# Last attention unit of a fused attention and long-convolution kernel: VectorE's queue reordered, four softmax products and one weight rest moved to GpSimd

## The reference

```python
h = einsum('bct,bcd->bdt', x, weights[condition])       # mixes the 32 channels
q_c = h @ Wq_c.T + bq_c;  q = (q_c @ Wq_up.T + bq_up)    # 32 heads of 128 + 64
kv = h @ Wkv_c.T + bkv_c                                 # latent 64 + rope 64
k_nope, v = split(kv[..., :64] @ Wkv_up.T + bkv_up)
attn = softmax(q . concat(k_nope, k_rope) / sqrt(192))   # 32 x 32 per row and head
x = x + (attn @ v) @ Wo.T, summed over the heads, + bo
y = mask * (causal_convolution(mask * x, kernel_of_channel) + D * mask * x)
x = x + y @ dequantized(qweight).T + bias
```

## Time and profile before

| | us |
|---|---|
| median of 3 timed runs | 732.34 (731.35 to 732.41) |
| the profiled execution, its own time | 729.96 |
| its span, first to last instruction | 728.1 |
| PE busy | 705.8 (97%) |
| VectorE busy | 601.3 (83%) |
| ACT busy | 412.7 (57%) |
| GpSimd busy | 208.1 (29%) |

### The profile page before, as it was taken

How to read it: one execution, slowest core, us unless ns; L and a number is a source line. 1 busy time by engine, 2 the same in 40 slices (tenths; PEclk the granted TensorE clock), 3 DMA queues, 4 the chain that set the end, 5 groups by cost and what they waited for, 6 DMA issues and landing times.

```text
span 728.1 us, 17041 instructions
## 1 busy us (share of the span) xinstructions
PE 705.8 (97%) x7154; PEld 567.8 (78%) x7154; DVE 601.3 (83%) x1010; ACT 412.7 (57%) x736; POOL 208.1 (29%) x237
## 2 busy tenths in 40 slices
PE   8999999999999999999999999999988899999997
PEld 6867777786978697777878786978666688888885
DVE  4889999998999777797769776787889689999975
ACT  4676565656556765746475565656645444444443
POOL 5461020020002010640110000004300257777784
PEclk9999999999999999999999999999999999999999
DMA  7800100010002001000100010002112487989943
GB/s 225 322 3 2 58 7 1 2 62 3 1 2 62 3 2 49 11 5 13 59 5 1 2 59 2 2 1 92 59 60 54 121 234 147 187 236 196 238 104 109
DMA packets 31919, 50.94 MB, mean 70 GB/s; under 512 B 6594, under 2 KB 21090, under 8 KB 30562
## 3 DMA queue, kind: packets, MB, share of 16 engines
q1 hardware_dynamic: 29858, 49.26, 25.0%
q0 software_dynamic: 1024, 0.53, 0.3%
q10 hardware_dynamic: 960, 0.06, 0.1%
HBM read 41.19 MB, written 8.63 MB: 68 GB/s over the span
## 4 chain that ended last, share of the span: by engine, by line
PE 72%; DVE 15%; issue 4%; ACT 4%; DMA 3%; POOL 2%; SPq 0%; DVEq 0%; ACTq 0%; POOLq 0%
PE ps L729 32%; PE ps L778 6%; PE ps L621 5%; PE ps L622 5%; PE ps L623 5%; PE ps L800 4%; PE ps L670 3%; PE ps L629 2%; PE ps L631 2%; PE ps L630 2%; DVE x_low L1654 2%; DVE x_t L1648 2%; PE ps L1022 1%; PE ps L1030 1%; DMA x_t<-in_x_channels 1%
## 5 line engine op out<-in xcount | busy, mean ns | idle before, releaser
L1134 ACT ACTIVATE qt<-ps,m_bias 128x512 f32<-128x512 f32 x228 | 145.9, 687 | 87.7 <-PE ps L729 86.9
L729 PE MATMUL ps<-q_high,m_high 64*128 64x512 f32 x768 | 165.0, 397 | 0.0
L729 PE MATMUL ps<-q_high,m_low 64*128 64x512 f32 x768 | 161.3, 387 | 0.0
L729 PE MATMUL ps<-q_low,m_high 64*128 64x512 f32 x768 | 113.8, 387 | 0.0
L729 PEld LDWEIGHTS ps<-q_high,m_high 64*128 64x128 f32 x768 | 88.7, 184 | 15.0 <-issue 5.5
L729 PEld LDWEIGHTS ps<-q_high,m_low 64*128 64x128 f32 x768 | 88.8, 184 | 9.2
L1422 DVE TENSOR_TENSOR z_low<-ps,z_high 128x512 fp32r<-128x512 f32 x128 | 79.8, 683 | 18.1 <-ACT z_high L1154 16.5
L729 PEld LDWEIGHTS ps<-q_low,m_high 64*128 64x128 f32 x768 | 81.1, 184 | 10.2
L1154 ACT CAST z_high<-ps 128x512 fp32r<-128x512 f32 x128 | 66.8, 597 | 14.6 <-PE ps L800 9.8
L1139 ACT ACTIVATE sc<-sc 128x512 f32<-128x512 f32 x60 | 38.1, 635 | 41.5 <-DVE sc L1407 41.4
L494 POOL TENSOR_TENSOR o_sum<-o_part,o_part 128x512 f32<-128x512 f32 x7 | 9.1, 1300 | 173.2 <-ACT o_part L1164 173.2
(11 more groups left out here) (259 smaller groups left out, 1468.7 us busy)
## 6 DMA issues: line engine op xcount, KB each, us to landing
x_raw<-in_x_groups SPq DMA_DIRECT2D x32, 256.0 KB, 4.0
x_t<-in_x_channels SPq DMA_DIRECT2D x8, 1024.0 KB, 7.9
out<-rest SPq DMA_DIRECT2D x32, 256.0 KB, 6.3
toep_high<-taps_scratch SPq DMA_DIRECT2D x32, 192.0 KB, 4.5
toep_low<-taps_scratch SPq DMA_DIRECT2D x32, 192.0 KB, 4.9
w_raw<-in_w_groups SPq DMA_DIRECT2D x8, 512.0 KB, 7.5
toep_far<-taps_scratch SPq DMA_DIRECT2D x32, 64.0 KB, 5.7
rope_raw<-in_rope_rows SPq DMA_DIRECT2D x8, 192.0 KB, 7.4
```

The costliest lines, as they stand in the source:

```text
L729: mm = pe.matmul(ps[:, fold_bank(u, j) + e, :], weights[rows, (GH * g + j) // 2, c, :], moving[c][rows, :], start=start, stop=stop)
L1134: act.activation(qt[:, j, :], ps[:, fold_bank(u, j) + j % 2, :], ACT.Identity, bias=m_bias[:, h:h + 1]).then_inc(s["qt_done"], 1)
```

## The change

On VectorE, ended_last is split into summed_last (sum and reciprocal) and turned_last (only the transpose, which now waits for the product by norm_done). Quarter 1 is begun directly behind quarter 0, and the other pieces are put in a new order. The four products, and woT_low in front of them, are made by GpSimd. On ACT, heads 8 and 9 are evicted before the exponential of quarter 0, and heads 10 and 11 before that of quarter 1. PE's and SP's programs are the same.

```diff
--- before.py
+++ after.py
@@ -586,6 +586,13 @@
                 pool.wait_ge(s["wfT_done"], k + 1)
             front(LAST - 1)
             pool.memset(f(ones_r[:]), 1.0).then_inc(s["ones_ready"], 1)
+            pool.wait_ge(s["woT_high_done"], 1)
+            pool.tensor_tensor(woT_low[:], woT_raw[:], f(woT_high[:]), ALU.subtract).then_inc(s["woT_done"], 1)
+            for q in range(4):
+                pool.wait_ge(s["inv_done"], 4 * LAST + q + 1)
+                pool.tensor_tensor(sc_last[:, q], sc_last[:, q],
+                                   row_stat[:, q, :].unsqueeze(2).broadcast_to([P, 4 * (GH // 4), C]),
+                                   ALU.mult).then_inc(s["norm_done"], 1)
             pool.wait_ge(s["oh_early"], 1)
             pool.tensor_tensor(o_low[0][:, :, 0:EARLY], o_sum[:, 0:4, 0:EARLY], f(o_high[0][:, :, 0:EARLY]),
                                ALU.subtract).then_inc(s["ol_early"], 1)
@@ -1277,11 +1284,10 @@
                         latent(u // 2)
             fold(LAST, 0, 4)
             part_taken(LAST - 2)
-            fold(LAST, 4, 8)
+            fold(LAST, 4, 10)
             soft_last(0)
-            fold(LAST, 8, 10)
+            fold(LAST, 10, 12)
             soft_last(1)
-            fold(LAST, 10, 12)
             values(LAST - 1, 0, 0, 4)
             fold(LAST, 12, 16)
             values(LAST - 1, 1, 0, 2)
@@ -1599,31 +1605,34 @@
                 dve.wait_ge(s["max_done"], n)
                 dve.tensor_tensor(last_rows(q), last_rows(q), last_wide(q), ALU.subtract).then_inc(s["sub_done"], 1)
 
-            def ended_last(q):
+            def summed_last(q):
                 n = 4 * LAST + q + 1
                 dve.wait_ge(s["exp_done"], n)
                 dve.tensor_reduce(last_stat(q), last_rows(q), AX.X, ALU.add).then_inc(s["sum_done"], 1)
                 dve.wait_ge(s["sum_done"], n)
                 dve.reciprocal(last_stat(q), last_stat(q)).then_inc(s["inv_done"], 1)
-                dve.wait_ge(s["inv_done"], n)
-                dve.tensor_tensor(last_rows(q), last_rows(q), last_wide(q), ALU.mult).then_inc(s["norm_done"], 1)
-                dve.wait_ge(s["norm_done"], n)
+
+            def turned_last(q):
+                dve.wait_ge(s["norm_done"], 4 * LAST + q + 1)
                 dve.transpose(pT_last[q][:].rearrange("p n a c -> p (n a c)"), q_flat(q)).then_inc(s["turn_done"], 1)
 
-            dve.wait_ge(s["woT_high_done"], 1)
-            dve.tensor_tensor(woT_low[:], woT_raw[:], f(woT_high[:]), ALU.subtract).then_inc(s["woT_done"], 1)
             begun_last(0)
-            ended_last(0)
             begun_last(1)
+            summed_last(0)
             values(LAST - 1, 0, 0, 4)
-            ended_last(1)
+            summed_last(1)
+            turned_last(0)
             begun_last(2)
+            turned_last(1)
             values(LAST - 1, 1, 0, 4)
             begun_last(3)
-            ended_last(2)
+            summed_last(2)
             values(LAST, 0, 0, 1)
-            ended_last(3)
-            values(LAST, 0, 1, 4)
+            summed_last(3)
+            turned_last(2)
+            values(LAST, 0, 1, 3)
+            turned_last(3)
+            values(LAST, 0, 3, 4)
             values(LAST, 1, 0, 4)
             dve.wait_ge(s["oh_done"], 1)
             dve.scalar_tensor_tensor(out=o_low[0][:, :, EARLY:].rearrange("p c b -> p b c"),
```

## The result

The kernel with the change takes **727.75** (median of 7 runs, 724.31 to 730.09), the kernel before beside it 731.1 (730.58 to 732.41, 7 runs). The two medians are 3.35 apart. The ratio, which is estimated from all runs and is not the quotient of the medians, is 0.9943 [0.9926, 0.996]: 4.2 us of 731.1, with an interval of 2.9 to 5.4. So the kernel is faster, and the 3.75 forecast lies inside the interval. The profiled execution took 725.95 (4.0 less than before) at a span of 724.0 (4.1 less).

What follows compares the result with a forecast made beforehand. PE was taken as the bound, its instructions unchanged, so only its waits could shrink: −2.85 − 0.90 = −3.75, other terms 0. From a median of 732.34 this gave 728.6, range 727.1 to 730.6.

Steps and rivals of the forecast that it cites:

- Term 1: PE's wait before unit 14's values (542.87): quarter 1 transposed earlier on VectorE removes the whole idle, −2.85 us.
- Term 2: PE's wait before the last unit's third scores (547.23): ACT evicting heads 8 and 9 earlier removes it, −0.90 us.
- Term 3: PE's smaller waits, 0.77 before 551.38 and 0.32 before 556.91, move along with PE and stay; nothing to gain.
- gap without event: 0.76 us at 558.13 in which PE waits for no event; may vanish or double, part of the forecast's spread.
- Term 4: woT_low made on GpSimd, wanted by PE at 573.13: costs 0, bound 0.2 us.
- Term 5: Four products on GpSimd at about 1.30 us instead of 0.69, covered by VectorE's other work: costs 0.
- Term 6: VectorE and GpSimd instructions holding each other up in the last unit: costs 0, upper bound 1.8 us.
- Term 7: The last part, from the first output projection, begins at 569.38 and stays as long, 155.0 us.
- Second cause: Rival: PE's first stall also waits for another semaphore, so only 0.90 is gained: 731.4; chance 0.05.
- given back: Rival: DMA sets the last part's pace and the gain is lost there, time stays 732.3; chance 0.04 to 0.06: 0.06.
- Slower by long products: Rival: long GpSimd products delay the turns of quarters 1 and 3, 734.2 at 5.5 us each; chance 0.04.
- 2D − 5.35: Loss in us for product duration D, from late turns of quarters 1 and 3; eats the gain at 4.55.

Runs made afterwards that it cites:

- before, no dummies: The kernel before the change, without its six dummy matmuls (they compute nothing that is used): 730.24, ratio 1.0007 to the kernel before.
- three times: The change with each of the four GpSimd products made three times: 729.71, ratio 0.9998 to the kernel before.
- four times: The change with each of the four GpSimd products made four times: 736.88, ratio 1.0074 to the kernel before.
- GpSimd only: The change with VectorE's and ACT's old order, GpSimd still making the four products and woT_low: 730.61, ratio 1.0005 to the kernel before.
- order only: The change with its new order kept, but the four products and woT_low returned to VectorE: 727.04, ratio 0.9954 to the kernel before.
- without dummies: The change with all six dummy matmuls taken out: 725.05, ratio 0.992 to the kernel before.

## Why the prediction was right, and where it was not

**Term 1, first stall, −2.85: right.** The transpose of quarter 1 came at 538.29 (538.2 forecast), the values of unit 14 at 540.05 (540.02) without idle time. Between starts it is 11.50 to 8.58, −2.92; the 0.07 more are the modelled end of the fold, which reaches beyond the next start when nothing waits. A start should have been set against a start.

**Term 2, second stall, −0.90: the size right, the reason wrong.** z_low started at 542.45, as forecast, and PE at 543.45 (543.48). But this is the step of the prediction that failed: "ACT had been late: it sat until 538.91 for the exponential of quarter 0 with heads 8 and 9 queued behind it", with the gain put down to ACT's new order. What stood ahead of z_high in the kernel before was the exponential of quarter 1, for which ACT was idle for 3.41 with heads 10 and 11 queued behind it:

```profile
544.10 0.63 ACT L1143 ACTIVATE sc_last<-sc_last 128x512 f32<-128x512 f32 x1 [3.41 <-DVE sc_last L1600]
544.64 1.25 ACT L1134 ACTIVATE qt<-ps,m_bias 128x512 f32<-128x512 f32 x2
```

It was late because VectorE transposed quarter 1 only at 541.94. That transpose now comes 3.65 earlier, and with ACT's old order only 0.17 of the 0.90 is lost: VectorE's new order is enough. Whether ACT's new order alone would be enough too was not run. By an estimate from these rows it would: z_high would follow the exponential at 544.64 instead of 545.78, 1.14 earlier, and the stall was 0.90. The prediction moved both queues at once and credited one.

**Term 3, what stays: right.** 0.77 and 0.35 stand (0.77 and 0.32 before). The gap without event was 0.51 instead of 0.76, which gave 0.25. It was 0.25 to 1.05 over all runs that had it, the old order's included (0.40 and 0.25), so this 0.25 can't be put down to the change; the prediction named it as a spread.

**Term 4, woT_low, 0: right** (37.38 with it on VectorE).

**Term 5, products, 0: right, the size off.** 1.05 instead of 1.30, all four covered. GpSimd's part of the change is worth 0.9 to 1.0 all the same, at two places that the sum did not need to price: VectorE is behind by its products at 554 and 562 without it.

**Term 6, collisions, 0: right in this order.** The subtraction of quarter 2 stood at 547.73, after the product's end at 545.90 + 1.05 = 546.95, and took 0.69. Turns and z_low beside a product took 0.65 to 0.71. With each product doubled a subtraction did meet one:

```profile
548.84 0.89 DVE L1610 TENSOR_TENSOR sc_last<-sc_last,row_stat 128x512 f32<-128x512 f32 x1
```

```profile
548.14 1.05 POOL L597 TENSOR_TENSOR sc_last<-sc_last,row_stat 128x512 f32<-128x512 f32 x1
```

GpSimd had 549.19 − 548.84 = 0.35 left, and VectorE lost 0.20. So the price is at most the overlap, and not a whole product. The Trainium skill ("SBUF — State Buffer", "Who interferes with whom") calls the port pair that VectorE and GpSimd share an exclusive lock. The traces agree: all but about 0.14 of the overlap is lost, and only where both of VectorE's inputs are in SBUF.

**Term 7, last part: right,** 154.94 for 155.0.

**The sum** was undersized in the profiles: −3.75 against −4.17, of which 0.13 are modelled ends, 0.25 the gap without event, 0.04 small differences. The timed runs don't tell it from 3.75: 3.35 by the first medians, 4.2 and 4.5 by the two ratios (0.9943 and 0.9939), with intervals of 2.9 to 5.4 and 3.4 to 5.6. The step that is missing is the clock: "nothing in it is a matter of the clock" is true of the one profiled execution, and was taken for all of them. The fall behind the same stall in "before, no dummies" cost 0.6; how much of the timed gain is clock is not shown. That 727.75 came within 0.9 of the forecast of 728.6 is in part luck: the forecast hung on the first three runs' median of 732.34, with four more runs before is at 731.1, and the change was at 725.83 when it ran again.

**The rivals.** Second cause and given back: not there. *Slower by long products* did not occur, but the runs show its formula wrong. 2D − 5.35 assumed each product to start at its reciprocal. GpSimd's queue makes quarter 3 wait for two products in a row, and PE's idle then took the clock. At three times (about 3.3 each) the formula gives a loss of 1.25, measured 4.04, and the whole gain is gone; at four times (4.5) it gives 3.65, measured 8.36. The point from which it is slower than before lies near 3.3, not at 4.55. (By its own formula D = 5.3 is 1.50 beyond the gain, not 1.46.)

## What to carry to other kernels

When a stall ends with an engine that is busy in a queue of its own, first move the one instruction that is waited for ahead of what nobody waits for; here the new order gave 3.3 of 4.2, while moving work to another engine alone gave nothing, and gave its 0.9 only once other work stood between hand-over and use. Set starts against starts, and test an attribution between two reordered queues by putting one back. A long idle of PE can cost more than its length, in some executions only, so look at the granted clock of many and not of one profile.

## What was not expected of the hardware

- **A product with a broadcast operand is shorter on GpSimd:** 1.05 (row_stat read with one value for 32 columns) against 1.30 for two full tensors of the same 128x512, in every run unless a VectorE instruction with both inputs in SBUF stood beside it. It is not the operation: L506 multiplies two full tensors and takes 1.29, and L499 multiplies two broadcast ones and takes 1.16 (mean ns, kernel with the change):

```profile
L506 POOL TENSOR_TENSOR o_sum<-o_sum 128x512 f32<-128x512 f32 x4 | 5.2, 1292 | 36.7 <-ACT o_sum L1129 36.7
L499 POOL TENSOR_TENSOR o_sum<-parT,pos 128x512 f32<-128x512 f32 x4 | 4.6, 1160 | 0.2
L593 POOL TENSOR_TENSOR sc_last<-sc_last,row_stat 128x512 f32<-128x512 f32 x4 | 4.2, 1052 | 20.1 <-DVE row_stat L1613 20.1
```
- **The hold between VectorE and GpSimd is the overlap less about 0.14, in both directions.** VectorE second: 0.35 left, 0.20 lost (above); 1.23 left (598.97 − 597.74), 1.10 lost, 1.78 for 0.68. GpSimd second: woT_low at 532.81 took 1.59 for 1.30 while a VectorE product of unit 14 ran until 533.25, 0.44 left, 0.29 lost:

```profile
532.37 0.88 DVE L1421 TENSOR_TENSOR sc<-sc,row_stat 128x512 f32<-128x512 f32 x1
```
- **The clock fell with idle times of 1.9, 2.0 and 3.3, and with one of 2.84 in one profiled execution, but not with 2.85 and 2.64 in two others** (before, and GpSimd only: clock 1.00 from 540 to 550 in both), and not with 1.0 (order only) or 0.8 (without dummies). Rows of the same form take 0.63 instead of 0.39 while it is down. What decides between the cases of 2.6 to 2.9 stays open.
- **The gap without event** inside the first values of the last unit was 0.25 to 1.05, and it was missing in the three runs in which the wait ahead of it was 0.78 or more (order only, three and four products). Its cause was not tried.
